# A hybrid layer on one Trainium2 core: another opening, a shorter addition at two tiles, and new orders on all engines

## What is computed

```python
x = x + attention(_layernorm(x), W_q)        # q = x W_q'; (q x') x, without a softmax
x = x + ffn(_layernorm(x), ...)              # relu(x w1 + b1) w2 + b2, residual, LayerNorm with gamma, beta
x = x + rwkv(_layernorm(x), ...)             # time mix (a decayed running softmax over tokens) and channel mix
x = x + ffn(_layernorm(x), ...)              # the same ffn once more
```

## Time and profile before

| | |
|---|---|
| time, median of 3 runs | 283.79 us (283.71 to 286.62) |
| the profiled execution's own time | 286.06 us |
| its span, first to last instruction | 284.3 us |
| mean granted TensorE clock | 0.981 |
| TensorE busy | 263.8 us (93%), 1556 instructions |
| ScalarE busy | 229.8 us (81%), 443 |
| VectorE busy | 227.1 us (80%), 739 |
| GpSimd busy | 148.5 us (52%), 294 |

### The profile page before, as it was taken

How to read it: one execution, slowest core, us unless ns; L and a number is a source line. 1 busy time by engine, 2 the same in 40 slices (tenths; PEclk the granted TensorE clock), 3 DMA queues, 4 the chain that set the end, 5 groups by cost and what they waited for, 6 DMA issues and landing times. The chain is left out here.

```text
span 284.3 us, 5322 instructions
## 1 busy us (share of the span) xinstructions
PE 263.8 (93%) x1556; PEld 196.6 (69%) x1556; DVE 227.1 (80%) x739; ACT 229.8 (81%) x443; POOL 148.5 (52%) x294
## 2 busy tenths in 40 slices
PE   7598999997996999999999999999999989999990
PEld 7598688566684577477665676866757848777770
DVE  1648616889999999999999999999998499754224
ACT  2486994966598989997999998998999998788630
POOL 3474934654192599285882661953922524851331
PEclk9959999999999999999999999999999999999997
DMA  6910340220124122244404303225351405643132
GB/s 185 310 53 0 56 81 15 40 37 13 24 39 75 26 51 37 39 76 74 74 1 77 74 16 60 37 47 105 55 108 26 75 0 110 115 98 78 25 61 74
DMA packets 17740, 18.10 MB, mean 64 GB/s; under 512 B 1456, under 2 KB 11568, under 8 KB 17712
## 3 DMA queue, kind: packets, MB, share of 16 engines
q0 software_dynamic: 6480, 11.80, 24.3%
q1 hardware_dynamic: 11232, 5.97, 7.4%
HBM read 3.87 MB, written 2.10 MB: 21 GB/s over the span
## 5 line engine op out<-in xcount | busy, mean ns | idle before, releaser
L961 PEld LDWEIGHTS bank<-W,f_h 128*128 128x128 f32 x512 | 61.3, 192 | 9.9 <-issue 9.2
L961 PE MATMUL bank<-W,f_h 128*128 128x128 f32 x512 | 63.1, 275 | 0.3 <-ACT f_h L738 0.3
L945 PE MATMUL bank<-f_yT,W 128*128 128x512 f32 x128 | 62.6, 599 | 0.1
L738 ACT ACTIVATE f_h<-bank,B1C 128x512 f32<-128x512 f32 x64 | 42.5, 684 | 9.5 <-PE bank L945 9.3
L1003 PE MATMUL bank<-XK,FWk 128*128 128x512 f32 x64 | 32.2, 607 | 2.8 <-DVE XK L559 1.4
L945 PEld LDWEIGHTS bank<-f_yT,W 128*128 128x128 f32 x128 | 21.7, 190 | 18.3 <-issue 12.3
L1009 PEld LDWEIGHTS bank<-FWv,KK 128*128 128x128 f32 x256 | 30.5, 192 | 4.8 <-issue 2.2
L1009 PE MATMUL bank<-FWv,KK 128*128 128x128 f32 x256 | 31.2, 276 | 0.2 <-ACT KK L799 0.2
L394 DVE BATCH_NORM_STATS2 f_zn_stats<-bank 128x6 f32<-128x128 f32 x64 | 14.1, 282 | 18.3 <-PE bank L961 18.2
L678 ACT ACTIVATE f_y<-R,f_yn_nb,f_yn_rs 128x128 f32<-128x128 f32 x64 | 26.3, 485 | 2.6 <-POOL f_yn_nb L297 2.3
L440 DVE SCALAR_TENSOR_TENSOR f_zg<-bank,f_zn_rs,GAMMA 128x128 f32<-128x128 f32 x64 | 17.9, 341 | 7.6 <-issue 5.6
(11 more groups left out here) (133 smaller groups left out, 619.2 us busy)
## 6 DMA issues: line engine op xcount, KB each, us to landing
R<-BETA POOLq DMA_DIRECT2D x16, 256.0 KB, 3.5
R<-f_zg POOLq DMA_DIRECT2D x14, 256.0 KB, 3.4
R<-in_hidden SPq DMA_DIRECT2D x8, 256.0 KB, 4.7
R<-N POOLq DMA_DIRECT2D x8, 256.0 KB, 3.3
out_x<-R SPq DMA_DIRECT2D x8, 256.0 KB, 2.3
R<-G POOLq DMA_DIRECT2D x7, 256.0 KB, 3.4
W<-in_w SPq DMA_DIRECT2D x2, 256.0 KB, 4.5
BETA<-in_beta SPq DMA_DIRECT2D x1, 256.0 KB, 5.2
```

Of the source, the lines that this page charges most:

```text
L738: a.activation(at(f.h, b)[:, n, :], banks[bank][:], ACT.Relu, bias=B1C[:, n:n + 1]).then_inc(f.h_ready[n], 1)
L945: t_.matmul(banks[bank][:], W1[:, n * P:(n + 1) * P], at(f.yT, b)[:], start=True, stop=True).then_inc(f.h_psum[n], 1)
L961: last = t_.matmul(banks[bank][:, j * C:(j + 1) * C], at(f.h, b)[:, n, j * P:(j + 1) * P], W2[:, n, :], start=False, stop=(n == H - 1), sk ...
```

## The change

1. Opening on TensorE: 24 warm-up transposes, `centre_bias`, 20 more, in place of 42 and then `centre_bias`. `centre_down_bias` comes later in VectorE's list.
2. Tile 0 is normalised for the attention by VectorE (a new `attn_normed`, four TENSOR_SCALAR) and not by ScalarE.
3. The load of tile 3 comes before B1 and W1.
4. `ffn_scaled` and `ffn_add` become `ffn_gain` (gamma times the product, one instruction of 512 columns) and `ffn_out` (scale and sum in four instructions that write `R`), for tile 0 of f1 and tile 7 of f2.
5. The scale steps and the back steps have two semaphores instead of one, the `xn_ready` steps three; `y` has three copies instead of two. Some waits are written anew to suit (`Rows.before`).
6. The lists of all four engines are new.

```diff
-COPIES = {"N": 3, "f1_y": 2, "f2_y": 2, ...}
+COPIES = {"N": 3, "f1_y": 3, "f2_y": 3, ...}
+SPLIT = {"f1": (0,), "f2": (7,)}
...
-                self.scale = Steps(n + "_scale_steps", 1, *steps)
+                self.scale = Steps(n + "_scale_steps", 2, *steps)
...
-                    self.ready = Steps(dst_name + "_ready", 1, "but last", "all")
+                    self.ready = Steps(dst_name + "_ready", len(dst) if n == "attn" else 1, "but last", "all")
...
-        back = Steps("back_steps", 1, "ve1", "tmp", "rs1", "back")
+        back = Steps("back_steps", 2, "ve1", "tmp", "rs1", "back")
...
             load_x0(2)
+            load_x0(3)
             sp.dma_start(B1[:], b1).then_inc(w1_loaded, DMA)
             sp.dma_start(W1[:], w1).then_inc(w1_loaded, DMA)
-            load_x0(3)
...
+            def ffn_gain(b, f, bank):
...
+                v.tensor_tensor(at(f.zg, b)[:], bank_rows(bank), GAMMA[:].unsqueeze(1).broadcast_to([P, J, C]), ALU.mult).then_inc(f.zg_ready, 1)
+
+            def ffn_out(b, f):
+
+                dve.wait_ge(*f.znorm.scale.done(b, "rs"))
+                dve.wait_ge(f.zg_ready, b + 1)
+                dve.wait_ge(*f.xb.ready(b))
+                for j in range(J):
+                    last = v.scalar_tensor_tensor(R[b][:, j, :], at(f.zg, b)[:, j, :], f.znorm.rs[b % 2][:, j:j + 1], R[b][:, j, :],
+                                                  ALU.mult, ALU.add)
+                last.then_inc(*f.out.step(b))
...
-            def ffn_add(b, f, tile):
-
-                dve.wait_ge(f.zg_ready, b + 1)
-                dve.wait_ge(*f.xb.ready(b))
-                v.tensor_tensor(R[b][:], at(tile, b)[:], R[b][:], ALU.add).then_inc(*f.out.step(b))
...
+            def attn_normed(b):
+
+                dve.wait_ge(na.mv_ready, b + 1)
+                dve.wait_ge(*na.scale.done(b, "rs"))
+                dst = at(XN, b)
+                for j in range(J):
+                    done = v.tensor_scalar(dst[:, j, :], R[b][:, j, :], na.mv[b % 2][:, j, 0:1], na.rs[b % 2][:, j:j + 1], ALU.subtract, ALU.mult)
+                    if j == J - 2:
+                        done.then_inc(na.ready.sem(b), 1)
+                done.then_inc(na.ready.sem(b), 1)
...
-            warm_up(0, 42); centre_bias(); attn_transpose(0, 0); attn_gram(0, 1); attn_transpose(1, 2)
+            warm_up(0, 24); centre_bias(); warm_up(0, 20); attn_transpose(0, 0); attn_gram(0, 1); bias_part()
```

551 lines of the change are left out of this document (284 added, 267 removed).

## The result

| | before | changed |
|---|---|---|
| time, median | 283.78 us (4 runs, 283.71 to 286.62) | 269.62 us (4 runs, 268.16 to 273.29) |
| ratio to before | | 0.947 (0.940 to 0.954) |
| profiled execution | 286.06 us, span 284.3 | 273.29 us, span 271.5 |
| predicted | | 273.0 us, range 270.0 to 281.0 |

The change makes the kernel 5.3% faster. Those are two kinds of execution: six more runs of the changed kernel gave 270.6 twice and 274.3 to 274.9 four times, with a median of 274.31 and a ratio of 0.959 (0.952 to 0.966). So the number to explain is not one but two, 268 to 271 and 273 to 275, and the profile shown here is of the second kind.

What follows compares the result with a forecast made beforehand. VectorE's early idle time, its dense work to XK of tile 5, TensorE's work behind it, then the tail: 42.8 + 153.5 + 0.9 + 63.4 + 3.9 + 6.7 = 271.2 span, with 1.76 around it 273.0 us; range 270 to 281.

Steps and rivals of the forecast that it cites:

- The opening: Start to first scan: TensorE waits 0.5 us at tile 1, first FFN product 20.7, first scan 42.8, VectorE idle 13.2.
- The price of the clock: TensorE from 13.8 to 20.6 us: the low clock loses about 3.3 us before; the new opening avoids it.
- normalising tile 0 on VectorE gains nothing: Opening: tile 0 ready at 7.5 instead of 8.5 us, but the warm-ups still end near 9.0, so no gain.
- A microsecond of idle VectorE before the dense part is a microsecond at the end: Before the first scan: VectorE's idle time counts in full at the end; 13.2 us instead of 25.2.
- The dense part: First scan to XK of tile 5, paced by VectorE: 153.5 us instead of 156.0.
- TensorE behind XK of tile 5: From there to TensorE's end: 0.9 hand-over, 63.4 as before, plus 3.9 us for added products.
- The tail: Behind TensorE's end: 6.7 us instead of 7.4, gain product hidden in a wait, four fused pieces 1.12.
- The one in which VectorE waits for ScalarE: Dense part: six waits of 2.35 us make 14.1, giving 287.1; chance 0.07 of no visible change, 0.07 slower.
- The clock did not fall behind the warm-up: Rival for the opening: TensorE's clock falls all the same, costing up to 3.3 us, so 276.3; chance 0.08.
- No difference carried over from profile to median: The profiled run before is 2.3 us above its median; the forecast kept no such difference for the new kernel.

Runs made afterwards that it cites:

- a4: Changed kernel with tile 6 of f2 also added by VectorE, without its adding transfer on GpSimd's queue: median 272.89 us, profiled run 268.32.
- a3: Changed kernel with one GpSimd step moved, the bias of tile 3 of f2 right behind its power: 269.64 us.
- a5: Changed kernel with both the bias step moved as in a3 and tile 6 of f2 added by VectorE as in a4: 268.94 us, ratio to before 0.945.
- b3: The kernel before, nothing edited, run again for a profile of its quicker group: 283.35 us.
- a9: Kernel of a3 with tile 0 normalised for the attention by ScalarE again, not by VectorE: 270.29 us.
- b2_opening: Kernel before with only the b2 product moved inside the warm-up and its subtraction behind tile 1's statistics and aggregation: 281.75 us, ratio 0.992.
- a7: Kernel of a3 with 16 unread statistics added on VectorE right behind the differences of tile 0: 273.99 us.
- a10: Kernel of a3 with one product up of tile 2 in f1 done five times instead of once on TensorE: 272.88 us.
- a8: Kernel of a3 with the 16 unread VectorE statistics placed late, behind the last gate product of tile 7: 273.90 us.
- a13: Changed kernel, nothing edited, run again for a third profile: 273.54 us.
- a6: Kernel of a3 with the b2 step as before (44 transposes, then the b2 product): median 273.15 us, profiled run 269.67.
- a11: The same kernel as a6, run again for a second profile: 271.46 us.

## What in the prediction was right, and which step failed

| term | predicted | profiled run | without the stall (a4; a3 for the tail) |
|---|---|---|---|
| first FFN product | 20.7 | 20.77 | 20.4 (a5) |
| first scan | 42.8 | 43.27 | 42.82 |
| first scan to XK of tile 5 | 153.5 | 153.47 | 150.26 |
| from there to TensorE's end | 68.2 | 66.25 | 66.24 |
| tail | 6.7 | 8.5 | 7.8 |
| span | 271.2 | 271.5 | 267.1 (sum) |

- **The opening: right.** Idle time before tile 1's transposes 0.40 (0.5 predicted), clock at 1.00, first FFN product and first scan within 0.5 us. VectorE's idle time ahead of the scan is 14.0 where I had 13.2. The price of the clock, 3.3 us, holds for executions like the profiled one; most runs of before lose less (b3). One statement was wrong: that normalising tile 0 on VectorE gains nothing; it is worth 0.3 to 0.7 us (a9).
- **A microsecond of idle VectorE before the dense part is a microsecond at the end: right** in b2_opening (4.5 at the scan, 3.2 at the end, the rest lost to the clock on the way) and in a7. It was too narrow, since TensorE's work counts as much now (a10), and VectorE's does so even late (a8).
- **The dense part: the failed step.** The prediction's 153.5 carried the old 3.3 us of VectorE's idle time along and had 150.2 of work. Measured are 149.2 of work in both kinds of execution, and idle time of 1.0 us (a4) or 4.25 (the profile). So the step that failed is carrying the old 3.3 us of idle time into the new order; 1.0 is what that order has by itself. That the sum met the profiled run within 0.3 us is luck: a new stall of 3.5 us stood where I had carried 3.3 of old waits, and the errors of the next two terms, 2.0 too much and 1.8 too little, nearly cancel. The lower end of my range took just these 3.3 off and stopped at 270.0; the median needed them off and the next term's 2.0 as well, less about 1 for the tail.
- **TensorE behind XK of tile 5: 2.0 too much.** The added instructions are the 18 that I counted (403 against 385 from its first channel-mix product of tile 5 on), but they lengthened its busy time by 2.8 us (62.36 to 65.19), not 3.9, and its idle time there fell from 1.1 to 0.3.
- **The tail: 1.8 too little in the profiled run, 1.0 in a3 and a13.** VectorE's part was right in size (1.14 for the four pieces, 1.12 predicted; the 0.78 estimated from a formula is too low). I had left out SyncE's order: the store of tile 7 stands behind that of tile 6, which waits for a transfer that landed 5.1 us after its issue (4.4 in a3 and a13). In the earlier trace rows nothing of this shows, since there the addition ended after that transfer had landed.
- **The rivals.** The one in which VectorE waits for ScalarE is what the stall looks like on VectorE (`G` from ScalarE, 3.49), once in the program and not once a tile; but its cause stands one engine further, on GpSimd, which I had costed nowhere. The clock did not fall behind the warm-up in any of the three profiles of the changed kernel; the warm-up itself varies (24 transposes in 4.93 to 5.38 us there), and the first scan with it (42.84 to 43.27).
- **No difference carried over from profile to median: half right.** The clock that separates the two in the kernel before (b3) is gone. The changed kernel has its own two kinds of run, for another reason.

What the gain is made of, without the stall and against b3, both of the quicker kind: 11.1 us by the first scan (53.92 to 42.82), 5.7 between it and XK of tile 5 (155.96 to 150.26), then 2.0 lost for more TensorE work behind it and 0.4 for the stores: 14.4, where the medians differ by 14.2. Of the 5.7, 2.5 are VectorE's work moved behind XK, as counted, 2.3 its old waits, and 0.9 stays unexplained. Of the opening, the b2 step alone brings 1.8 us to the scan against b3 (4.5 against the profiled run, the clock in it); step 2 brings 0.3 to 0.7 (a9). Most of the rest should be work of other tiles moved from ahead of the scan to behind it, since TensorE's busy time ahead of it fell from 48.4 (b3) to 41.3 us; no run here separates it further.

## What to carry to other kernels

When an order is packed so that three engines are busy about 97% or more, look at the small steps of the fourth. GpSimd was busy 60% of the span, yet a 0.2 us product queued behind two others set all engines back by 3 us, in three of three profiles and, by the times, in six of eleven executions: put the step that somebody waits for right behind its own input, ahead of those that nobody waits for yet. For the end of a kernel, follow the stores through their queue too, not only the engine that computes last. And before two profiles are compared, line them up at the same instruction: a microsecond between them can come from a warm-up or from one slow step, and not from the edit.

## What the runs showed of the hardware

- GpSimd's 128x4 products take 4.56 us for twelve beside VectorE additions with two SBUF inputs, 4.73 beside TENSOR_SCALAR from SBUF, and 1.86 beside additions with a PSUM input or statistics. VectorE's own pace did not change (3.70 and 3.68 for six).
- The same three steps of GpSimd, beside the same instructions of VectorE, take 1.5 us in one execution and 5.5 in another (from 182.81 in a4, from 182.91 in the changed kernel), and with them the kernel takes 268 or 273 us. Another power takes 1.60 or 2.20 us in two profiles of one kernel (a6, a11). What decides is not shown.
- The same 42 transposes at the start took 6.67, 7.49 and 7.71 us in three profiles of one program; with TensorE idle 3.0 us behind them in all three, the granted clock from 13.8 to 20.6 was 0.86, 0.51 and 0.54. Idle times of 1.64 to 1.95 us at that place gave 1.00 twice and 0.82 once. An idle time of 1.94 us later in the program was followed by 32 narrow products at 1.00 in 3.74 us (before) and at 0.67 in 5.36 (b2_opening).
- The last adding transfer of 256 KB landed 5.1 and 5.2 us after its issue in two profiles of the changed kernel and 4.4 in the third, where 3.4 is the median of the fourteen of its kind.
